# A transformer layer on eight cores: weights cast to bf16 ahead of time in HBM, or on their way into SBUF

## What is computed

```python
q  = hn @ Wq.T                                   # hn = layernorm(x), 32 heads of 128
kc, vc = hn @ Wk_down.T, hn @ Wv_down.T          # 8 heads of 32 each
lat = concat([kc, vc], -1).reshape(b, s, 512)
k_cmp, v_cmp = split(lat, 2, -1)
k, v = k_cmp @ Wk_up.T, v_cmp @ Wv_up.T          # 8 heads of 128, each used by 4 query heads
out = softmax(causal(q k^T / sqrt(128))) v @ Wo.T
x = x + layernorm(out)
xf = layernorm(x)
base = xf @ base_W.T
gate = softmax of the 2 largest of xf @ gate_W.T  (28 experts), scattered to 28 columns
h = einsum('nd,erd->ner', xf, lora_A) * (2 * gate)[:, :, None]       # rank 8
x = x + layernorm(base + einsum('ner,eor->no', h, lora_B))
```

## Time and profile before

| | us |
|---|---|
| median of two timed runs (5231.4 to 5261.4) | 5246.4 |
| profiled execution | 5230.2 |
| its slowest core (7), first to last instruction | 5229.0 |
| its fastest core (0) | 5145.1 |

### The profile page before, as it was taken

One profiled execution on the slowest core, in us unless ns is written; L12 is line 12 of the kernel. 1 busy time (PEld: TensorE's weight loads), 2 busy tenths in 40 slices (PEclk: granted clock), 3 DMA queues, 4 the chain that ended last, 5 costly groups with the idle time before them and its releaser, 6 DMA issues.

```text
span 5229.0 us, 37005 instructions; the slowest of 8 cores (5145.1 to 5229.0 us)
## 1 busy us (share of the span) xinstructions
PE 3032.0 (58%) x13056; PEld 1197.6 (23%) x13056; DVE 1526.9 (29%) x2250; ACT 1029.2 (20%) x977; POOL 160.7 (3%) x230
## 2 busy tenths in 40 slices
PE   0202112020120597889992793797998999893694
PEld 0100001010010242323341341342332333341242
DVE  1011011010101213666314104114666666414103
ACT  0010001000001102545102001104554555202001
POOL 0100001000010100000000000000000000000000
PEclk9956556565665798999996796898999999996797
DMA  9999999999999854000362364643000000363364
GB/s 118 128 122 118 117 115 118 118 110 113 122 114 130 161 150 108 1 1 17 85 171 54 110 165 138 159 137 65 1 1 1 1 1 1 75 170 77 86 172 134
DMA packets 640433, 494.22 MB, mean 95 GB/s; under 512 B 417520, under 2 KB 626416, under 8 KB 626944
## 3 DMA queue, kind: packets, MB, share of 16 engines
q0 software_dynamic: 154560, 197.64, 32.2%
q1 hardware_dynamic: 485696, 294.23, 23.9%
HBM read 604.93 MB, written 121.63 MB: 139 GB/s over the span
## 4 chain that ended last, share of the span: by engine, by line
PE 53%; another core or an unknown queue 14%; DMA 11%; DVE 7%; SPq 6%; ACT 4%; issue 3%; DVEq 1%; POOLq 0%; POOL 0%; ACTq 0%
PE psz L455 7%; SPq L218 6%; PE pss L490 6%; PE psb L364 4%; PE psa L749 4%; PE psb L578 4%; PE psa L578 4%; PE psb L749 4%; PE psa L364 4%; DVE BSTAT L194 4%; DMA UFMA<-UTM 4%; PE psb L462 4%; PE psa L462 4%; PE psa L301 2%
## 5 line engine op out<-in xcount | busy, mean ns | idle before, releaser
L301 PE MATMUL psa<-UFMA,WPa 128*128 128x512 bf16 x512 | 142.8, 448 | 1460.4 <-DMA UFMA<-UTM 1395.6
L498 ACT ACTIVATE PTD<-pss 128x1024 bf16<-128x1024 f32 x768 | 740.9, 1021 | 659.4 <-PE pss L490 659.4
L504 DVE TENSOR_TENSOR PTD<-PTD,M 128x2048 bf16<-128x2048 bf16 x384 | 470.4, 1225 | 420.1 <-ACT PTD L498 420.1
L490 PE MATMUL pss<-QFM,KFM 128*128 128x512 bf16 x1536 | 404.0, 380 | 68.4 <-ACT PTD L498 45.7
L309 DVE CAST KCVC<-psa 128x512 bf16<-128x512 f32 x16 | 11.1, 691 | 1379.4 <-PE psa L301 1379.4
L301 PEld LDWEIGHTS psa<-UFMA,WPa 128*128 128x128 bf16 x512 | 56.0, 112 | 1546.7 <-issue 1507.4
L455 PE MATMUL psz<-PTD,E 128*16 128x512 bf16 x1536 | 395.7, 380 | 0.2 <-DVE ACC L477 0.2
L206 ACT ACTIVATE STAT<-STAT 128x1 f32<-128x1 f32 x64 | 12.9, 201 | 1766.2 <-DVEq L204 899.6
L364 PE MATMUL psa<-UFMA,WPa 128*128 128x512 bf16 x1024 | 230.4, 384 | 166.6 <-DMA WPa<-WQB 165.8
L749 PE MATMUL psa<-QFM,WPa 128*128 128x512 bf16 x1024 | 229.6, 383 | 28.4 <-DMA WPa<-BWBMB 28.4
L578 PE MATMUL psa<-QFM,WPa 128*128 128x512 bf16 x1024 | 230.1, 383 | 2.7 <-DVE QFM L528 2.2
(11 more groups left out here) (116 smaller groups left out, 2439.5 us busy)
## 6 DMA issues: line engine op xcount, KB each, us to landing
BWBMB<-BWBM POOLq DMA_DIRECT2D x32, 1088.0 KB, 86.9
XA<-X POOLq DMA_DIRECT2D x32, 1024.0 KB, 30.0
WQB<-WQ POOLq DMA_DIRECT2D x32, 1024.0 KB, 71.5
WOB<-WO POOLq DMA_DIRECT2D x32, 1024.0 KB, 74.8
WPa<-WKVD POOLq DMA_DIRECT2D x16, 1024.0 KB, 23.7
WPb<-WKVD POOLq DMA_DIRECT2D x16, 1024.0 KB, 28.6
OUT<-OSTG SPq DMA_DIRECT2D x16, 1024.0 KB, 4.1
XA<-XOWN POOLq DMA_DIRECT2D x8, 1024.0 KB, 20.8
```

What stands on the lines that cost most here:

```text
L301: ins = TEN.matmul(PSab[pp][:], WP[wp][:, c * 128:(c + 1) * 128], ubuf[:, c * 512:(c + 1) * 512], start=(c == 0), stop=(c == 31))
L490: ins = TEN.matmul(PSS[:, kt * 512:(kt + 1) * 512], KFM[:, kv4 * 512 + kt * 128: kv4 * 512 + (kt + 1) * 128], QFM[:, h * 512:(h + 1) * 512 ...
L498: ins = SCA.activation(PTD[:, ptp * 2048 + hf2 * 1024: ptp * 2048 + (hf2 + 1) * 1024], PSS[:, hf2 * 1024:(hf2 + 1) * 1024], AF.Exp, scale= ...
L504: pm = vS.inc(VEC.tensor_tensor(PTD[:, ptp * 2048:(ptp + 1) * 2048], PTD[:, ptp * 2048:(ptp + 1) * 2048], M01[:], AL.mult))
```

## The change

- The bf16 copies in HBM and the 128 conversions are gone. The weight loads of Q, O, ATP and FFN are issued by GpSimd instead of SP, read f32 and cast on the way into WP.
- WKVD4, WQ4, WO4, BWBM4 and GWT are laid out by the host so that each SBUF partition's share of a load is one contiguous row (16 KB of f32 for most) instead of 32 pieces of 512 bytes.
- The XA tiles become six instead of four, used in turn over all tiles; XA2 takes four tiles in the place of QFM.

```diff
-    WQ4 = nc.dram_tensor("WQ4", [32, 32, 128, 128], F32, kind="ExternalInput").ap()
+    WQ4 = nc.dram_tensor("WQ4", [32, 128, 4096], F32, kind="ExternalInput").ap()
...
-    WQB = nc.dram_tensor("WQB", [32, 32, 128, 128], BF16, kind="Internal").ap()
...
-    XA2 = A("XA2", [128, 2 * 4096], BF16, O_Q)
+    XA2 = A("XA2", [128, 4 * 4096], BF16, O_Q)
...
     def pa_loads(ub):
         for t4 in range(4):
-            sv, _ = free_xa[t4]
+            b = (ub * 4 + t4) % 6
+            sv, _ = free_xa[b]
             W(GPS, (sS, sv))
             src = Xr[t4 * 128:(t4 + 1) * 128, ub, :]
-            pend_xm[t4] = sXA[t4].inc(GPS.dma_start(out=xa_tile(t4), in_=src), 16)
+            pend_xm[t4] = sXA[b].inc(GPS.dma_start(out=xa_tile(b), in_=src), 16)
...
-            pump_conv(3)
...
             W(GPS, (tS, wp_free[wp]))
-            srcw = WKVD4[cg].rearrange("c p ch -> p c ch")
-            dstw = WP[wp][:, 0:32 * 128].rearrange("p (c ch) -> p c ch", c=32, ch=128)
-            wm = sWPs[wp].inc(GPS.dma_start(out=dstw, in_=srcw), 16)
+            wm = sWPs[wp].inc(GPS.dma_start(out=WP[wp][:, 0:32 * 128], in_=WKVD4[cg]), 16)
...
-        pump_conv(len(conv_jobs))
         for hdc in range(32):
             wp = hdc % 2
-            W(SYN, (tS, wp_free[wp]), (sCVQ, sCVQ.v))
-            srcw = WQB[hdc].rearrange("c p h -> p c h")
-            dstw = WP[wp][:, 0:32 * 128].rearrange("p (c h) -> p c h", c=32, h=128)
-            wm = sWPh[wp].inc(SYN.dma_start(out=dstw, in_=srcw), 16)
+            W(GPS, (tS, wp_free[wp]))
+            wm = sWPh[wp].inc(GPS.dma_start(out=WP[wp][:, 0:32 * 128], in_=WQ4[hdc]), 16)
...
-        gwf_ld = sGW[0].inc(GPS.dma_start(
-            out=GWPF[:].rearrange("p (c e) -> p c e", c=32, e=28),
-            in_=GWT.rearrange("c p e -> p c e")), 16)
+        gwf_ld = sGW[0].inc(GPS.dma_start(out=GWPF[:], in_=GWT[:]), 16)
...
-            W(SYN, (tS, max(wp_free[wp], wo_base_free)), (sCVO, sCVO.v))
...
+            W(GPS, (tS, max(wp_free[wp], wo_base_free)))
+            wm = sWPh[wp].inc(GPS.dma_start(out=WP[wp][:, 0:32 * 128], in_=WO4[oc2]), 16)
...
-            W(SYN, (tS, ap_free[ap2]), (sCVA, sCVA.v))
-            am = sAP[ap2].inc(SYN.dma_start(out=WP[0][:, ap2 * 256:(ap2 + 1) * 256],
-                                            in_=ATPB[c]), 16)
+            W(GPS, (tS, ap_free[ap2]))
+            am = sAP[ap2].inc(GPS.dma_start(out=WP[0][:, ap2 * 256:(ap2 + 1) * 256],
+                                            in_=ATP[c]), 16)
...
-            W(SYN, (tS, max(wp_free[wp], bl_base_free)), (sCVB, sCVB.v))
...
+            W(GPS, (tS, max(wp_free[wp], bl_base_free)))
+            wm = sWPh[wp].inc(GPS.dma_start(out=WP[wp][:], in_=BWBM4[oc2]), 16)
```

More of the change, by code:

```diff
@@ L141, in build @@
     gS = Sem(nc, "gS")
-    sXA = [Sem(nc, "sXA0"), Sem(nc, "sXA1"), Sem(nc, "sXA2"), Sem(nc, "sXA3")]
+    sXA = [Sem(nc, "sXA%d" % i) for i in range(6)]
     sWPs = [Sem(nc, "sWP0"), Sem(nc, "sWP1")]
@@ L228, in final_waits, with xa_tile @@
                 SYN.wait_ge(s.h, s.v)
-    conv_jobs = []
-    for i in range(32):
-        conv_jobs.append((sCVQ, WQB[i], WQ4[i]))
-    for i in range(32):
-        conv_jobs.append((sCVO, WOB[i], WO4[i]))
-    for i in range(32):
-        conv_jobs.append((sCVB, BWBMB[i], BWBM4[i]))
-    for i in range(32):
-        conv_jobs.append((sCVA, ATPB[i], ATP[i]))
-    cv_i = [0]
-    def pump_conv(n):
-        for _ in range(n):
-            if cv_i[0] >= len(conv_jobs):
-                return
-            s, d, srcp = conv_jobs[cv_i[0]]
-            s.inc(GPS.dma_start(out=d, in_=srcp), 16)
-            cv_i[0] += 1
     Xr = X.rearrange("(q0 eight) d -> q0 eight d", eight=8)
     xu_extra = []
-    free_xa = [(0, 0), (0, 0), (0, 0), (0, 0)]
-    def xa_tile(pb):
-        t = XA if pb < 2 else XA2
-        return t[:, (pb % 2) * 4096:(pb % 2 + 1) * 4096]
+    free_xa = [(0, 0)] * 6
+    def xa_tile(i):
+        if i < 2:
+            return XA[:, i * 4096:(i + 1) * 4096]
+        return XA2[:, (i - 2) * 4096:(i - 1) * 4096]
     utm_free = [0, 0]
@@ L570, in build @@
             wp = oc2 % 2
-            W(SYN, (tS, max(wp_free[wp], wo_base_free)), (sCVO, sCVO.v))
-            srcw = WOB[oc2].rearrange("c p h -> p c h")
-            dstw = WP[wp][:, 0:32 * 128].rearrange("p (c h) -> p c h", c=32, h=128)
-            wm = sWPh[wp].inc(SYN.dma_start(out=dstw, in_=srcw), 16)
+            W(GPS, (tS, max(wp_free[wp], wo_base_free)))
+            wm = sWPh[wp].inc(GPS.dma_start(out=WP[wp][:, 0:32 * 128], in_=WO4[oc2]), 16)
             pp = oc2 % 2
@@ L741, in build @@
             wp = oc2 % 2
-            W(SYN, (tS, max(wp_free[wp], bl_base_free)), (sCVB, sCVB.v))
-            srcw = BWBMB[oc2].rearrange("c p h -> p c h")
-            dstw = WP[wp][:].rearrange("p (c h) -> p c h", c=34, h=128)
-            wm = sWPh[wp].inc(SYN.dma_start(out=dstw, in_=srcw), 16)
+            W(GPS, (tS, max(wp_free[wp], bl_base_free)))
+            wm = sWPh[wp].inc(GPS.dma_start(out=WP[wp][:], in_=BWBM4[oc2]), 16)
             pp = oc2 % 2
@@ L816, in _host_layout @@
     kv = kv.reshape(512, DM)
-    WKVD4 = C(kv.T.reshape(32, 128, 4, 128).transpose(2, 0, 1, 3))
-    WQ4 = C(Wq.T.reshape(32, 128, 32, 128).transpose(2, 0, 1, 3))
-    WO4 = C(Wo.T.reshape(32, 128, 32, 128).transpose(2, 0, 1, 3))
+    WKVD4 = C(kv.T.reshape(32, 128, 4, 128).transpose(2, 1, 0, 3).reshape(4, 128, 4096))
+    WQ4 = C(Wq.T.reshape(32, 128, 32, 128).transpose(2, 1, 0, 3).reshape(32, 128, 4096))
+    WO4 = C(Wo.T.reshape(32, 128, 32, 128).transpose(2, 1, 0, 3).reshape(32, 128, 4096))
     wku = Wku.T.reshape(4, 64, 1024)
@@ L827, in _host_layout @@
     WVUDO = C(np.concatenate([zv, wvu], axis=1).transpose(1, 0, 2).reshape(128, 4 * 1024))
-    bw4 = bW.T.reshape(32, 128, 32, 128).transpose(2, 0, 1, 3)
+    bw4 = bW.T.reshape(32, 128, 32, 128).transpose(2, 1, 0, 3)
     Bmat = lB.transpose(1, 0, 2).reshape(DM, 224)
@@ L831, in _host_layout @@
     BmT[0:224, :] = Bmat.T
-    bm4 = BmT.reshape(2, 128, 32, 128).transpose(2, 0, 1, 3)
-    BWBM4 = C(np.concatenate([bw4, bm4], axis=1))
-    GWT = C(gW.T.reshape(32, 128, NE))
+    bm4 = BmT.reshape(2, 128, 32, 128).transpose(2, 1, 0, 3)
+    BWBM4 = C(np.concatenate([bw4, bm4], axis=2).reshape(32, 128, 34 * 128))
+    GWT = C(gW.T.reshape(32, 128, NE).transpose(1, 0, 2).reshape(128, 32 * NE))
     ATf = np.zeros((DM, 256), np.float32)
```

25 lines of the change are left out of this document (8 added, 17 removed).

## The result

The changed kernel takes 4854.3 us (median of 12 executions, 4819.9 to 5000.0) where the kernel before took 5256.2 beside it (10 executions); the ratio is 0.924, 95% interval 0.920 to 0.927. The forecast was 4470 us with a range up to 4690. The direction was right, the size was not: of the 762 us forecast to go, about 400 went.

A forecast was written before the change was run, and what follows sets the result against it. The prediction took the latent stage as DMA-bound by weight conversions and the other stages as matmul-bound. From 5230 us, -1114 (latent), -6 (chain into Q) and +358 (streams, O's start, ATP) gave 4468, stated as 4470; range 4290 to 4690.

The forecast's parts named there:

- What bounds the kernel now, conversions gone: Latent stage: DMA-bound by weight conversions; without them 54 us of DMA work in a 76 us block, -1114 us.
- The chain of a latent block, 40 us: Latent stage, first statistics to first matmul of a block: 40 us, bounds 35.3 and 45.
- The 67 and 85 us a block: Latent stage: low and high block times around 76 us, changing the stage by -1186 or -1042 us.
- Rival 4: Latent stage stays DMA-late: transposes keep taking 24 us, chain 63 us instead of 40, 4654 us; chance 0.06.
- The matmul part of a block, 35.4: Latent stage: a block's four matmul groups, with a 3.1 us gap for a load, copy and start, take 35.4 us.
- The streams, landing 9.0: Q, O, FFN: GpSimd weight loads land in 9.0 us, setting rounds of 8.56, 8.81, 9.18; +46, +57, +54 us a chunk.
- rival 2: Weight streams: idle gaps cost the clock, each matmul burst paying 1.68 us, +161 us, 4631 us; chance 0.12.
- Rivals 1 and 3: Streams: every landing 10.4 under shared HBM, 4628 us, chance 0.15; or landing 6.0 to 6.4, hidden, 4220, chance 0.07.
- the prediction's estimate from that: Weight loads with both cores of a pair streaming: transfer 5.9 us instead of 5.0, about 90 us longer.
- O's start, +12: Start of O after attention: WO's first load waits in GpSimd's queue behind GWT, so TensorE waits, +12 us a chunk.
- ATP, 4.4 us a pair: ATP: pairs of rounds go from 3.26 to 4.4 us with a 2.7 us landing, +19, net +10 us a chunk.
- Chunk 0's chain, 38: Chunk 0's chain from latent stage into Q: 38 us instead of 44.2, -6 us.

The follow-up runs named there:

- e5_keepconv: Kernel before with only the host's contiguous weight layouts, conversions kept: 5283.9 us median against 5382.9 for before beside it.
- e8_micro2: Transfers alone, no layer computed, in the latent stage's time order: early-load groups 40 to 45 us, late ones with four loads 46 to 90.
- e1_micro: Transfers alone, no layer computed, neither loads nor transposes waiting for the other: four casting loads 29.2 us on core 3, 41.4 with four transposes.
- e3_order: Changed kernel with all latent loads placed under matmuls, none beside the transposes: 4579.7 us median.
- e12_all: Changed kernel plus latent loads under matmuls, third Q/O/FFN weight buffer, O/FFN loads and FFN's first load waiting for transposes, four ATP buffers: 4368.4 us, ratio 0.839.

## Why the prediction failed, step by step

- *What bounds the kernel now, conversions gone.* Half right: the DMA-bound stretch shrank, and e5_keepconv shows that the conversions and not the layout held it. But "54 us, so DMA is no longer the bound" was wrong: the engines were busy for 0.94 of the stage.
- *The chain of a latent block, 40 us, "bounds 35.3 (cover holds) and 45 (11 + 34, DMA-bound)".* **This step failed**, and carries 365 of the 379 us. The upper bound took DMA work as additive: four loads and four transposes, each at the price of its quiet row. e8_micro2 shows that sum to hold when loads come first (40 to 45 us with 8 of marks) and e1_micro when they fall between two transposes (41.4), e3_order shows the lower bound to be reachable (35.6), and the kernel's own order is outside both (94): its loads began while a transpose was in flight. A sum of quiet rows was no bound for a contended case. The 67 and 85 us a block that the range was built from follow from no sum in the text; its own bounds give 71 and 80.
- *Rival 4, chance 0.06.* The nearest: it said that a transpose keeps taking a long time beside packets of the software queue, and that tile 2 then waits for tile 0's transpose. The mechanism was this one; I priced the transpose with a landing of 24 us, and on core 5 the first stood in the way for 64. Its "against", only 54 us of DMA work in 76, counts bytes and was the same mistake again. The traces of before could have warned: in the earlier trace rows WKVD lands in 23.7 us, which I put down to the conversions wholly, and over the latent stage of before the 132096 packets of the transposes' queue had 0.184 of the engines' time, 0.184 x 16 x 1735.8 / 132096 = 39 ns each, where in the earlier trace rows a transposing packet takes 18.
- *The matmul part of a block, 35.4.* Right (37.4).
- *The streams, landing 9.0.* Right in the main: landings 8.6 to 9.8, rounds 8.79, 8.57 and 9.33 against 8.56, 8.81 and 9.18 (its own terms add to 9.16 for the last). The 0.5 us that O's landing was to gain from its transposes did not come: 8.6 and 8.9. TensorE's clock fell from 0.99 to 0.96 in them, so rival 2 (gaps cost the clock) is true for a small part: 236.5 us of matmul in Q against 224.6, 12 us more where 32 slow bursts would be 54; half of it, 6 us, falls on the time by the rival's own sum, and Q took 7 us more than forecast. Rivals 1 and 3 did not come: no landing as long as 10.4 in the median, none as short as 6.4.
- *What the Trainium skill would make of the landing.* By the Trainium skill (HBM Reference, section Specifications (TRN2)) a core gets about 358 GB/s when both cores of a pair stream; the prediction's estimate from that, 0.9 us of transfer more, would make landings 9.9. WQ's are 8.2 to 8.7 on the eight cores, at a mean demand of 2.1 MB in 8.8 us or 240 GB/s, so no run here shows the limit. By the Trainium skill (DMA: Bandwidth & Descriptors, section Latency and other measured facts) GpSimd's first byte comes 0.4 us behind SP's, which by itself would make the landing 6.4, an estimate; the trace does not agree.
- *O's start, +12.* Right, 11.60 us of wait:

```profile
1848.28 0.55 POOL L540 DMA_DIRECT2D WPa<-WO  x1
...
1857.57 2.72 PE L544 MATMUL psa<-QFM,WPa 128*128 128x512 bf16 x6 [11.60 <-DMA WPa<-WO]
```

- *ATP, 4.4 us a pair.* 74.4 / 16 = 4.65, from a landing of 3.3 us where I took 2.7; on this core the term was 4 us a chunk too small. On cores 0, 2, 4 and 6, with landings of 2.3 and 2.4, it was 8 us too large (62). e12_all shows that four buffers halve it.
- *Chunk 0's chain, 38.* 41.4; 3 us too hopeful.

## What stays open

Why a transposing packet goes from 18 to hundreds of ns when a load begins beside it is not visible in a trace. What the traces do show is that it outlasts the loads' bulk: 640 ns a transposing packet over 24 us in which a seventh of the load packets ran, and 18 ns once the last had landed. The list of what does it (f32 loads of either queue, casting loads in long rows, bf16 of GpSimd's queue at times) and what did not (bf16 without conversion of ScalarE's queue, but for a group or two; casting loads in quarters at 4 KB of f32 a row; and, the one kind tried so, four casting loads in long rows that begin before the first transpose) fits no single rule that I tried: not the conversion, the queue, the tensor read, the bytes in all, and not the size of a piece alone. Within one kind, the time of a group varied by a factor of two between cores and passes.

## What to carry over

When transposing transfers and weight loads share the DMA engines, don't price them by the sum of their quiet rows alone: look for stretches where the engines are full and the rate is a tenth of the usual, and ask which transfer began inside which. Look at when the packets begin and not at the order in the program: in e1_micro the loads that stand first went out second. Put loads ahead of the transposes or under matmuls; where they must run beside them, cut converting loads into pieces of a quarter row, which cost GpSimd 2.1 us of issuing for each load of 1 MB and brought 4% in the changed kernel. Buffers added to a stream pay only once this is settled: the same third buffer took a stage without transposes from some 270 to 223 us, beside transposes it gave up to 407 on some cores, and with cut loads, in the one trace there is, all it promised.
